# Middle layer: 25 counted blocks with four gathered entries beside each in place of 23 with six, and one of a group's four one-hots made by ACT

## What is computed

```
h   = x @ W
out = zeros.at[dst].add(h[src] * dinv[src] * dinv[dst]) + b
```

## Time and profile before

| | |
|---|---|
| median of 3 runs | 5629.05 us (5628.74 to 5634.06) |
| the profiled execution, its own time | 5619.51 us |
| its span | 5617.7 us |
| mean granted PE clock | 0.764 of 2.4 GHz |
| busy | PE 87%, DVE 74%, POOL 66%, ACT 46% of the span |
| the touched phase, first one-hot to last addition | 2430 to 3282 us of the span |

### The profile page before, as it was taken

The page is one execution under the profiler, slowest core; times in us unless marked ns, Lnnn a source line. Parts: engine busy times, 40 slices in busy tenths (PEclk is TensorE's granted clock), DMA queues, the critical chain, the costliest instruction groups (busy, mean ns, idle before and its releaser), DMA issues. The chain is left out here.

```text
span 5617.7 us, 135125 instructions
## 1 busy us (share of the span) xinstructions
PE 4864.0 (87%) x31642; PEld 3763.6 (67%) x31642; DVE 4130.7 (74%) x13322; ACT 2580.8 (46%) x6777; POOL 3708.4 (66%) x3867
## 2 busy tenths in 40 slices
PE   3999999999999997869989876999999999999993
PEld 3666666666666664447777754777777777777773
DVE  5888888888888886767777764666666666666667
ACT  1666666666666663133333343333333333333336
POOL 2777777777777772056666625777777777777772
PEclk7999999999999998978888875555555555555555
DMA  6555555555555553321111112222222222222231
GB/s 164 149 147 147 148 148 148 148 146 148 148 148 148 148 148 105 98 50 46 44 46 46 44 26 46 54 54 54 54 54 54 54 54 55 54 55 54 54 51 49
DMA packets 531415, 504.32 MB, mean 90 GB/s; under 512 B 328647, under 2 KB 390672, under 8 KB 531023
## 3 DMA queue, kind: packets, MB, share of 16 engines
q0 software_dynamic: 122832, 255.14, 19.9%
q1 hardware_dynamic: 337654, 130.31, 10.6%
q10 hardware_dynamic: 70794, 117.58, 6.6%
HBM read 476.98 MB, written 25.63 MB: 89 GB/s over the span
## 5 line engine op out<-in xcount | busy, mean ns | idle before, releaser
L1808 POOL DMA_INDIRECT Gt<-TAB,metat x1632 | 1554.9, 953 | 617.9 <-issue 496.5
L599 POOL DMA_INDIRECT G<-Atab,ms x1616 | 1539.3, 953 | 524.6 <-issue 484.9
L1978 PE MATMUL SR<-P,Gt 128*128 128x64 f32 x3264 | 804.0, 428 | 0.0
L1294 POOL DMA_INDIRECT Gc<-XS,metac x560 | 536.2, 957 | 345.1 <-issue 185.6
L1978 PEld LDWEIGHTS SR<-P,Gt 128*128 128x128 f32 x3264 | 727.3, 328 | 47.8
L736 PE MATMUL Z<-WB,ZR 96*128 96x128 f32 x3232 | 450.8, 283 | 189.3 <-DVE EE L622 126.0
L1842 DVE SCALAR_TENSOR_TENSOR M<-neqt,Gt 128x128 f32<-128x128 f32 x816 | 204.0, 291 | 515.0 <-DMA Gt<-TAB,metat 515.0
L1916 ACT ACTIVATE sc<-df 1x64 f32<-1x64 f32 x408 | 104.2, 256 | 1005.8 <-DVE df L1877 851.9
L736 PEld LDWEIGHTS Z<-WB,ZR 96*128 96x128 f32 x3232 | 394.1, 192 | 242.3 <-issue 111.3
L674 ACT ACTIVATE EE<-EE 128x512 f32<-128x512 f32 x404 | 254.7, 631 | 647.7 <-DVE EE L622 643.4
L1439 ACT COPY acc<-CP 128x300 f32<-128x300 f32 x690 | 295.1, 428 | 523.5 <-PE CP L1477 522.9
(11 more groups left out here) (285 smaller groups left out, 9722.4 us busy)
## 6 DMA issues: line engine op xcount, KB each, us to landing
mm<-MM ACTq DMA_DIRECT2D x202, 512.0 KB
ZR<-in_eft SPq DMA_DIRECT2D x202, 256.0 KB
Gt<-TAB,metat POOLq DMA_INDIRECT x1632
tb<-DF SPq DMA_DIRECT2D x202, 128.0 KB
G<-Atab,ms POOLq DMA_INDIRECT x1616
dq<-DQ SPq DMA_DIRECT2D x12, 768.0 KB, 5.9
Gc<-XS,metac POOLq DMA_INDIRECT x560
ad<-ADT SPq DMA_DIRECT2D x408, 0.5 KB
```

Source lines behind the costliest of these rows:

```text
L599: e.indirect_dma_start(G[:, k, s, :], None, Atab, bass.IndirectOffsetOnAxis(ap=ms[:, k, s:s + 1], axis=0)).then_inc(l_g[k], 16)
L1294: e.indirect_dma_start(G[:, k, s, :], None, XS, bass.IndirectOffsetOnAxis(ap=meta[:, k, s:s + 1], axis=0)).then_inc(l_g[k], 16)
L1808: e.indirect_dma_start(G[:, k, s, :], None, TAB, bass.IndirectOffsetOnAxis(ap=meta[:, k, s:s + 1], axis=0)).then_inc(l_g[k], 16)
L1978: m = e.matmul(SR[q][:, 0:2 * W], G[:, k, s, 0:128], P[:, q, s * 2 * W:(s + 1) * 2 * W], start=(s == 0), stop=(s == 3))
```

## The change

Three things are edited. The number of counted blocks goes from 23 to 25, so the counted nodes from 4140 to 4500. The entries beside a block go from six to four; the due groups become 0, 7, 15 and 22. And O1 of the second half (t = 1) is no longer made by DVE but by ACT, in two activations: `apart` writes |VA - i| for column i, 128 columns in float32, to one of two buffers `away`, and `onehot` writes Relu(1 - away) to O1 in bfloat16. ACT makes them ahead of its copies: in the step of group w it makes the one-hot of group w + 2 and the distance of w + 3. New semaphores s_aw and s_m2 count them; PE waits for s_m2 as well before a group's matmuls, and ACT waits for PE's group w - 2 before it writes over O1's slot.

```diff
-ND = 23
+ND = 25
-JB = 6
+JB = 4
...
+        away = sbt(ph, "away", [128, 2, 128])
...
+        one = v["ones"][:, 0:1]
...
             def pair(k, t, w):
-                e.tensor_scalar(O1[:, k, t, :], iotaD[:, 0:128], VA[:, 1, t, ds(w, 1)], None, ALU.is_equal)
+                if t == 0:
+                    e.tensor_scalar(O1[:, k, t, :], iotaD[:, 0:128], VA[:, 1, t, ds(w, 1)], None, ALU.is_equal)
                 return e.tensor_scalar(O2[:, k, t, :], iotaD[:, :], VA[:, 0, t, ds(w, 1)], None, ALU.is_equal)
...
+            e.wait_ge(s_va, 2 * NR)
+            e.wait_ge(s_io, 3)
+
+            def apart(w, k):
+                wait(e, s_m2, w - 1)
+                e.activation(away[:, k % 2, :], iotaD[:, 0:128], ACT.Abs, bias=VA[:, 1, 1, ds(w, 1)], scale=-1.0).then_inc(s_aw, 1)
+
+            def onehot(w, k):
+                wait(e, s_aw, w + 1)
+                e.activation(O1[:, k % 4, 1, :], away[:, k % 2, :], ACT.Relu, bias=one, scale=-1.0).then_inc(s_m2, 1)
+
+            apart(0, 0)
+            apart(1, 1)
+            onehot(0, 0)
+            apart(2, 2)
+            onehot(1, 1)
...
                     w, q = w0 + j, (k0 + j) % 2
+                    if b or j >= 2:
+                        wait(e, s_pm, w - 1)
+                    onehot(w + 2, k0 + j + 2)
+                    apart(w + 3, k0 + j + 3)
                     wait(e, s_pm, w + 1)
                     e.copy(C[b % 2][:, :, j * WD:(j + 1) * WD],
...
                     wait(e, s_m1, w + 1)
+                    wait(e, s_m2, w + 1)
                     wait(e, s_ev, w + 1)
```

More of the change, by code:

```diff
@@ L1212, in phase_sum @@
         s_m1 = sem("c_m1")
+        s_aw = sem("c_aw")
+        s_m2 = sem("c_m2")
         s_pm = sem("c_pm")
```

## The result

The changed kernel takes 5689.90 us, the median of 4 runs (5688.56 to 5692.34), against 5631.56 us before (4 runs): the ratio is 1.0108, 95% interval 1.0096 to 1.0120. That is 58 us or 1.1% slower. The forecast was 5714 us, 85 us slower, with a range from 5660 to 5805.

A forecast was written before the change was run, and what follows sets the result against it. PE was taken to pace mid-block, with losses at block edges. Terms +72.2 - 42.7 - 10 + 60 - 12 + 11 + 4.5 + 1 = +84, taken as 85, gave 5705 us, 5714 against the median; range 5660 to 5805.

The forecast's parts named there:

- The path and the tail: Middle layer: PE paces mid-block; behind the last product, twelve more entries cost 48 gathers at 1.25 us, +60 us.
- Two more blocks less 48 entries less the moved one: Middle layer: blocks +72.2 us, entries gone -42.7, group 5's entry moved to group 7, mostly at the high clock, -10.
- ACT's part: One-hot moved to ACT: +11 us in groups without product, +4.5 first block, -12 at block edges, +1 head.
- the head's +1 us: Ahead of the first copy: row pointers of 751 groups instead of 691 and two activations, +1 us.
- Where there is no product, ACT is slower than DVE was: three groups a block: Groups without a product, 24 blocks: ACT needs 0.93 us a group against DVE's 0.78, +11 us.
- The -12 us for DVE's shorter refill: Block edge, groups 29, 0 and 1: PE waits 0.16 us less each for DVE's one-hots, half counted, -12 us.
- The threshold of 0.98 us: Groups with a product: ACT becomes the pace from 0.98 us a group, since PE needs 24.4 us over 25 groups.
- ACT as the pace: Rival, blocks: semaphore waits eat ACT's overlap, 1.08 us a group, +170 us in all, 5799 us; chance 0.19.
- the low clock for whole blocks: Rival: short PE gaps keep the clock low, product groups take 1.7 us, +575 us, about 6290 us; chance 0.03.
- table loads: Rival, ACT: table loads around Abs and Relu, 1.28 us each, x 1500, +1900 us; chance 0.01.
- a faster kernel: Rival: entries hold the edges and clock down, so blocks fall to 28.4 us, -53 us, 5576 us; chance 0.04.
- Edges get cheaper: Rival, block edges: low clock ends half as late and both small ACT costs are absent, 5660 to 5690 us; chance 0.08.

The follow-up runs named there:

- counts_only: The kernel before with 25 blocks and four entries beside each, all four one-hots still on DVE: 5700.31 us, ratio 1.0131.
- act_wide: The changed kernel with ACT's absolute value taken over 300 columns in place of 128: 5716.63 us, ratio 1.0154.
- act_one: The changed kernel with one ACT activation a group in place of two, absolute value left out, sums not the reference's: 5664.46 us, ratio 1.0062.
- loop4: The changed kernel with four blocks in a loop iteration in place of two: 5666.59 us, ratio 1.0067.
- peel4: The kernel before plus ACT's one-hot alone, with blocks 1 and 2 ahead of the loop and four blocks an iteration: 5590.95 us, ratio 0.9931.
- late_total: peel4 with the addition of OT moved from group 28 to group 2 of the next block: 5529.54 us, ratio 0.9819.

## Why the prediction was right, and where it was off

**The path and the tail: right.** That PE is the pace in mid-block, that fewer entries free PE only for their own 0.89 us, and that twelve more entries behind the last product cost 48 gathers x 1.25 us with nothing beside them: +60 us forecast, +60.5 in the profile, 56.5 taken back by the run without them. This one term is the result; everything else, +24 us in the forecast, cancels to within a few us in the traces.

**Two more blocks less 48 entries less the moved one (+19.5 us): 7 too much.** counts_only has this part without ACT's. It took 72.5 us where the term with tail and head gives 79 or 80. A block is 33.6 us where the sum has 33.9. The moved entry was sized rightly: copy to copy, groups 5 and 6 of a block take 3.46 us before and 2.15 in counts_only, 1.31 less for an entry that costs 0.89 elsewhere, so 0.42 us is the surcharge of the low clock at that place, just what I had taken. The other 0.3 us a block, 6 us in all, has no term in the sum: 0.2 of it is spread over groups 28 to 4. Its cause stays open.

**ACT's part (+11 + 4.5 - 12 + 1 = +4.5 us): the wrong sign.** Alone it is worth -16 us on 22 blocks; on top of the counts -10 us between the two medians, -14 with each against its own kernel before, and -7 by the rows of the two traces. The sign is the same in all of them. The first block was near (+3.2 us, forecast +4.5); the head's +1 us can't be checked, as said above. The step that failed is "Where there is no product, ACT is slower than DVE was: three groups a block", +11 us. ACT does take 0.89 us a group there, and copy 4 comes 0.4 us later behind copy 1 than before. But the first product, on group 4, gives all of it back: groups 1 to 4 together take 3.93 us before, 3.90 in counts_only and 3.75 after. I had let ACT catch up at the entries, and overlooked that it also does so at the product after those groups and at the stop of group 28 (2.58 us in counts_only, 2.29 after). act_wide shows the same, with half of the price a block that I had worked out. act_one shows what the 0.89 still costs against a DVE that has three one-hots and needs 0.62: groups 1 to 4 take 3.18 us there. The -12 us for DVE's shorter refill was right in kind: PE's wait behind `total` is 1.38 us where it was 1.57, and groups 28, 29 and 0 together take 6.38 us after where counts_only has 6.75, 9 us over the 24 blocks.

**ACT's cost: nearly right.** 0.93 us a group forecast from three rows of other phases, 0.89 measured; each activation 0.40 as forecast, and no table load. The threshold of 0.98 us can't be confirmed as a sharp one: at 1.03 us the loss is 0.9 us a block where I had 1.9, and with one activation (act_one; 0.89 - 0.30, an estimate of 0.59 us a group) the gain is 0.8, nearly all of it in groups 1 to 6.

**The difference between 85 and 58 us.** The rows of the two traces give +66 us in the phase and 3 behind it, where the sum has +84. Of these 18 us, 6 are the counts and 12 are ACT's part. The other 11 us between +69 by the profiled executions and +58 by the medians come from the execution that I worked from: it was 12 us below the median of its kernel's four runs, the one of after 1 us below. I had added 10 us for this to the base, and not asked whether the phase had a part in it; no trace of a second execution shows where they lie.

**Rivals.** ACT as the pace, the low clock for whole blocks, table loads and a faster kernel didn't come. "Edges get cheaper" came in part: the measured 5690 us stands on the border between it and the forecast. The time lies well inside the range because the tail makes nearly all of the change; the terms beside it were too dear together, and none of them was needed for that.

## What to carry to other kernels

Work that is moved off a stage where one engine is the pace saves only that engine's share of it; ask first where the work that no longer fits goes, and whether anything runs beside it there. Four slots of gathers ahead hid little in this tail: twelve more entries cost the full issue time of their 48 gathers. And when a stage's bulk has no gaps, look at its edges: moving one addition by four groups gained 61 us, while the change that shifted work between three engines gained nothing in the blocks taken together (+4 us) and lost 60 behind them.

## What the runs showed of the hardware

- The end of a loop costs DVE 2.6 to 3.4 us of nothing, once an iteration, whether it holds two blocks or four. With four blocks ACT has a gap of its own there, 2.5 to 3.6 us (loop4, peel4), and it is the one that is left when DVE isn't held up by the stop at group 28 (late_total, 2.4 to 3.3 us).
- A stop of PE cost more than itself here, since the granted clock was 0.50 behind it: a loop's end is worth 3.5 us (loop4) where DVE idles 2.7. With the stop at `total` gone the mean granted clock in the blocks rose from 0.92 to 0.96 (peel4 to late_total).
- Two ACT instructions that follow each other overlap by 0.10 us even with a semaphore wait between them that is already met: 0.40 us each, 0.30 apart (2767.09 and 2767.39 in the changed kernel).
- In two sessions the same kernel took 7220 and 7363 us in place of 5630, and in the runs beside it DVE waited up to 5 us at a time for something that the trace doesn't hold. I don't know the cause, nor whether the chip is it. A ratio taken there isn't that of the other sessions.
